# Sixteen-wide attention: the causal mask of the scores for the row minima, added by VectorE in the instruction that takes the minimum

## What is computed

```python
q = _rope(q, cos, sin); k = _rope(k, cos, sin)     # HEAD_DIM = 16, N_HEADS = 32, N_KV = 8
k = jnp.repeat(k, Q_PER_KV, axis=2)
v = jnp.repeat(v, Q_PER_KV, axis=2)
mask = _blocksparse_mask(S)                        # S = 1024: all causal pairs
scores = jnp.einsum('bqhd,bkhd->bhqk', q, k) * SM_SCALE
scores = jnp.where(mask[None, None], scores, jnp.finfo(scores.dtype).min)
probs = jax.nn.softmax(scores, axis=-1)
ctx = jnp.einsum('bhqk,bkhd->bqhd', probs, v).reshape(B, S, HIDDEN)
out = jnp.einsum('bsh,oh->bso', ctx, w_dense) + b_dense
```

## Time and profile before

| | |
|---|---|
| median of 3 runs | 2730.2 us (2727.94 to 2735.07) |
| span of the profiled execution | 2730.3 us |
| opening with fills, loop of `L0a` | 45 to 113 us, 113 to about 345 us |
| the same of `L1b` | from 2020 us, loop until about 2330 us |
| TensorE, VectorE, ScalarE, GpSimd busy | 93%, 70%, 55%, 32% |
| VectorE's reductions at L825, each attention | 304, 186.4 us |

### The profile page before, as it was taken

The page is one execution under the profiler, slowest core; times in us unless marked ns, Lnnn a source line. Parts: engine busy times, 40 slices in busy tenths (PEclk is TensorE's granted clock), DMA queues, the critical chain, the costliest instruction groups (busy, mean ns, idle before and its releaser), DMA issues. The chain is left out here.

```text
span 2730.3 us, 42122 instructions
## 1 busy us (share of the span) xinstructions
PE 2526.2 (93%) x14520; PEld 1768.8 (65%) x14582; DVE 1919.6 (70%) x3384; ACT 1497.2 (55%) x2530; POOL 879.1 (32%) x816
## 2 busy tenths in 40 slices
PE   7899989879999999999999988899778999898995
PEld 5444446757888888888888865566554444465663
DVE  6878734558777777777777677677578787376775
ACT  4677832335555555555555542566446778425663
POOL 2200014245444353434435320355312000014552
PEclk9799999989999999999999998999987999999998
DMA  4000000010000000000000003988820000149888
GB/s 177 1 1 1 1 21 1 1 51 17 24 20 20 24 24 20 24 16 24 17 24 24 13 21 140 345 198 198 197 74 1 1 1 2 66 177 301 199 197 210
DMA packets 68719, 196.24 MB, mean 72 GB/s; under 512 B 8960, under 2 KB 9728, under 8 KB 63392
## 3 DMA queue, kind: packets, MB, share of 16 engines
q1 hardware_dynamic: 47456, 144.25, 15.5%
q0 software_dynamic: 21056, 49.30, 9.7%
HBM read 153.14 MB, written 40.37 MB: 71 GB/s over the span
## 5 line engine op out<-in xcount | busy, mean ns | idle before, releaser
L1489 ACT ACTIVATE L1a_ph<-single 128x512 fp32r<-128x512 f32 (+3 forms) x384 | 174.3, 489 | 181.2 <-PE single L1574 180.5
L1480 ACT ACTIVATE L1a_probs<-pair,L1a_least 128x128 f32<-128x128 f32 (+7 forms) x256 | 189.9, 744 | 73.3 <-DVE L1a_least L1623 72.2
L1629 DVE TENSOR_TENSOR L1a_pl<-single,L1a_ph 128x512 fp32r<-128x512 f32 (+3 forms) x384 | 199.5, 549 | 42.7 <-ACT L1a_ph L1489 42.1
L1645 DVE SCALAR_TENSOR_TENSOR x<-single,L1a_rinv,x 128x512 f32<-128x512 f32 x256 | 189.4, 745 | 56.9 <-PE single L1230 56.6
L1457 POOL TENSOR_TENSOR L1a_swapped<-L1a_swapped,L1a_sin 128x512 f32<-128x512 f32 x80 | 129.2, 1616 | 301.0 <-ACT L1a_swapped L1521 301.0
L1623 DVE TENSOR_REDUCE L1a_least<-pair 128x1 f32<-128x128 f32 (+7 forms) x256 | 190.7, 750 | 42.9 <-PE pair L1563 42.3
L825 DVE TENSOR_REDUCE L1b_least<-single 128x1 f32<-128x512 f32 (+3 forms) x304 | 186.4, 657 | 37.8 <-PE single L647 20.3
L825 DVE TENSOR_REDUCE L0a_least<-single 128x1 f32<-128x512 f32 (+3 forms) x304 | 186.4, 657 | 37.6 <-PE single L647 19.2
L528 ACT ACTIVATE L1b_probsT<-pair 128x896 f32<-128x896 f32 (+2 forms) x192 | 149.0, 811 | 59.5 <-PE pair L667 47.2
L528 ACT ACTIVATE L0a_probsT<-pair 128x896 f32<-128x896 f32 (+2 forms) x192 | 148.9, 811 | 59.6 <-PE pair L667 47.3
L1574 PE MATMUL single<-ident,L1a_probs 128*128 128x128 f32 x1152 | 169.0, 274 | 0.4 <-ACT L1a_probs L1480 0.4
(11 more groups left out here) (537 smaller groups left out, 7023.9 us busy)
## 6 DMA issues: line engine op xcount, KB each, us to landing
L1f_wd<-in_L1f_w SPq DMA_DIRECT2D x48, 512.0 KB
L1g_wd<-in_L1f_w SPq DMA_DIRECT2D x48, 512.0 KB
L1a_raw<-in_L1a_w SPq DMA_DIRECT2D x80, 256.0 KB, 2.6
L1f_store<-in_L1f_w SPq DMA_DIRECT2D x16, 1024.0 KB, 10.2
L1g_store<-in_L1f_w SPq DMA_DIRECT2D x16, 1024.0 KB, 10.3
sum<-L0a_pad_row SPq DMA_DIRECT2D x2, 2304.0 KB, 17.1
sum<-x SPq DMA_DIRECT2D x16, 256.0 KB
x<-sum SPq DMA_DIRECT2D x16, 256.0 KB, 6.7
```

Of the source, the lines that this page charges most:

```text
L1480: act.activation(probs[:, u % 2, 0:n], g.pair[u % 2][:, 0:n], ACT.Exp, bias=least[:, u % 4:u % 4 + 1], scale=-1.0, accum_out=rsum[:, h % 2 ...
L1489: act.activation(p_tile(ph, u, i), turned_bank(u, i), ACT.Copy).then_inc(p_high, 1)
L1629: dve.tensor_tensor(p_tile(pl, u, i), turned_bank(u, i), p_tile(ph, u, i).bitcast(F32), ALU.subtract)\
L1645: dve.scalar_tensor_tensor(out=g.x[:, t, :], in0=aux_bank(("O", h, t)), scalar=rinv[:, h % 2, t:t + 1], in1=g.x[:, t, :], op0=ALU.mult, op ...
```

## The change

A new constant `later`, 128 x 512 in bf16, is zero but for its last 128 columns, which hold the mask. GpSimd builds it beside the other constants. TensorE's `fill` no longer issues the mask matmul. In `lowest`, an unmasked fill is read as before. For a masked one VectorE issues, per head, `tensor_tensor_reduce`: it adds the last w columns of `later` to the head's w columns in PSUM, writes the sum back in place, and puts the minimum into `least`.

```diff
@@ constants
+                pool.memset(g.later[:, :], 0.0).then_inc(done, 1)
...
+                pool.affine_select(out=g.later[:, HALF - P:HALF], in_=g.later[:, HALF - P:HALF], compare_op=ALU.is_ge,
+                                   fill=BIG, base=0, pattern=[[-1, P]], channel_multiplier=1).then_inc(done, 1)
@@ fill
-                        masked = part == banks_of(qt) - 1
                         mm = pe.matmul(to[:, o:o + w], a.qkT[0:KS, kv * GH + first + i, qt * P:(qt + 1) * P],
-                                       a.qkT[0:KS, kv + NH, k:k + w], start=True, stop=not masked)
-                        if masked:
-                            mm = pe.matmul(to[:, o + w - P:o + w], g.ident_b[:, :], g.mask_b[:, :],
-                                           start=False, stop=True)
+                                       a.qkT[0:KS, kv + NH, k:k + w], start=True, stop=True)
@@ lowest
-                    dve.tensor_reduce(a.least[:, part, qt, first:first + heads],
-                                      g.bank(BANK16["F", kv, f])[:, 0:heads * w].rearrange("p (j k) -> p j k", j=heads),
-                                      AX_X, ALU.min).then_inc(a.fill_read, 1)
+                    held = g.bank(BANK16["F", kv, f])
+                    if part == banks_of(qt) - 1:
+                        for i in range(heads):
+                            j = first + i
+                            mm = dve.tensor_tensor_reduce(out=held[:, i * w:(i + 1) * w], in0=held[:, i * w:(i + 1) * w],
+                                                          in1=g.later[:, HALF - w:HALF], scale=1.0, scalar=BIG,
+                                                          op0=ALU.add, op1=ALU.min, accum_out=a.least[:, part, qt, j:j + 1])
+                    else:
+                        mm = dve.tensor_reduce(a.least[:, part, qt, first:first + heads],
+                                               held[:, 0:heads * w].rearrange("p (j k) -> p j k", j=heads), AX_X, ALU.min)
+                    mm.then_inc(a.fill_read, 1)
```

More of the change, by code:

```diff
@@ L86, in __init__ @@
         self.mask_b = sb("mask_b", [P, P], BF16)
+        self.later = sb("later", [P, HALF], BF16)
         self.stats = sb("stats", [P, NT, 6])
@@ L209, in _ @@
                 pool.memset(g.ones[:, :], 1.0).then_inc(done, 1)
-                pool.wait_ge(done, 3)
+                pool.memset(g.later[:, :], 0.0).then_inc(done, 1)
+                pool.wait_ge(done, 4)
                 pool.affine_select(out=g.ident[:, :], in_=g.ident[:, :], compare_op=ALU.not_equal, fill=1.0,
@@ L215, in _ @@
                                    base=0, pattern=[[-1, P]], channel_multiplier=1).then_inc(done, 1)
-                pool.wait_ge(done, 5)
+                pool.affine_select(out=g.later[:, HALF - P:HALF], in_=g.later[:, HALF - P:HALF], compare_op=ALU.is_ge,
+                                   fill=BIG, base=0, pattern=[[-1, P]], channel_multiplier=1).then_inc(done, 1)
+                pool.wait_ge(done, 7)
                 pool.tensor_copy(g.ident_b[:, :], g.ident[:, :]).then_inc(done, 1)
-                pool.wait_ge(done, 6)
+                pool.wait_ge(done, 8)
 def fills():
```

## The result

| | before | after |
|---|---|---|
| median of 6 runs each, same chip | 2731.8 us (2726.0 to 2735.8) | 2720.6 us (2714.0 to 2725.6) |
| ratio | | 0.9962, 95% interval 0.9944 to 0.9979 |
| span of the profiled execution | 2730.3 us | 2718.3 us |

The changed kernel is faster by 0.4%, some 11 us, where the forecast was no change. The page of the changed kernel, part 1, answers to the earlier trace rows: TensorE has 18 us less work and VectorE 31 us more. 512 mask matmuls are gone, as the rows of weight loads (PEld, 14582 to 14070) count them; the matmul rows show 450, because before some were missing from the records.

The account below looks back on a forecast made before the run. TensorE was taken to bound the loop by its own work, VectorE to end last in the opening. Loop, opening and constant summed to 2 x (-1.4 + 1.65) + 0.2 = +0.7 us on 2730.3: forecast 2731 us, range 2713 to 2760.

Parts of the forecast that it names:

- VectorE's rate: Masked fills: the combined instruction runs at full rate, 0.07 us + 1.04 ns a column.
- the half-rate rival: Masked fills: the combined instruction costs 1.04 ns a column more, about 2845 us; chance 0.07, shared with a falling clock.
- The accumulator read, r = 0.08: VectorE, per head of a masked fill: the second instruction, reading the accumulator, adds r = 0.08 us, range 0.05 to 0.20.
- The dear-read rival: Fill 6 and opening: accumulator read costs over 0.12 us; 2749 us at 0.15, 2768 at 0.20; chance 0.28.
- The crowded run: Loop, fills 0 to 6: TensorE waits for VectorE at fills 3 to 6, +0.45 us a period.
- The rest of a period: Loop, after the crowded fills to fill 35: TensorE sheds 1.04 us, of which 0.65 is gained.
- The loop as a whole: Each attention's loop: seven periods at -0.2 us, -1.4 us in all (-4.2 to +3.2).
- The opening: First group of each attention: VectorE ends last, so its dearer fills add +1.65 us (0 to +3.2).
- The join: Between group 0's last minimum and the first copy of values: the forecast sum has no term for it.
- a falling clock: TensorE's clock falls because TensorE pauses: a slower outcome, chance 0.07 together with half rate.
- The total: Whole kernel: +0.7 us on 2730.3, forecast 2731 us; chance of the forecast case 0.50.
- Faster: TensorE's bound rules everywhere: Loop: what TensorE sheds arrives, 13 us per attention; all gives 2704 us, two thirds 2713; chance 0.15.

Follow-up runs that it names:

- both_masks: The changed kernel with TensorE's mask matmul put back into the fills, so the mask is added twice: 2738.5 us, ratio 1.0018.
- wide_fills_only: The combined instruction only in fills holding one head (384 and 512 columns), the others keeping TensorE's mask matmul as before: 2720.1 us, ratio 0.996.
- narrow_fills_only: The combined instruction only in fills holding two or four heads, the others keeping TensorE's mask matmul as before: 2733.2 us, one run.
- no_mask_in_first_pass: The kernel before without the first pass's mask matmuls, softmax shift being half the minimum over unmasked scores: 2709.5 us, ratio 0.9919.
- experiment 6: The kernel before with the combined instruction in group 0 alone, or in fills 0 to 10 of group 1 alone: 2733.1 and 2725.4 us, one run each.
- combined_but_in_the_crowd: The changed kernel with TensorE's mask put back at fills 0 to 2 of groups 2 to 7 alone: 2709.4 us, ratio 0.9928.
- opening_only: The kernel before with the combined instruction in the fills of group 0 alone: 2733.1 us, one run.
- constant_only: The kernel before with the new constant `later` built by GpSimd and not used: 2731.2 us, ratio 1.0001.

## Why the prediction was right about the loop and wrong about the sign

**VectorE's rate: right.** Rows of about 282, 415, 550 and 685 ns were forecast; they are 322, 458, 591 and 707. The rows are longer where an accumulator read lies beneath the start of the next. The distances of starts are those of the full rate, and the half-rate rival is out. The groups of VectorE by shape (busy us, mean ns, idle before), in both parts of the attention `L0a`:

```profile
L829 DVE CUSTOM_DVE_ANT_0 single<-single,later 128x512 f32<-128x512 f32 x64 | 43.9, 707 | 6.7 <-PE single L647 6.5
L829 DVE DVE_READ_ACCUMULATOR2_ANT L0a_least<- 128x1 f32 x256 | 36.3, 142 | 0.0
...
L829 DVE CUSTOM_DVE_ANT_0 single<-single,later 128x128 f32<-128x128 f32 x64 | 16.6, 322 | 0.7 <-PE single L647 0.7
```

The Trainium skill (Vector Engine (DVE) Microarchitecture Reference, Measured stream behaviour on trn2) would give the accumulator read the same 75 ns as any instruction in a row; the trace has 0.05 us.

**The accumulator read, r = 0.08: mis-sized, too dear.** It is 0.05, the low end of the range. A fill of 4 x 128 went from 0.60 to 1.00 us (four steps of 0.25; forecast 1.12), 2 x 256 to 0.76 (forecast 0.83), a wide one by 0.05 (forecast 0.08). Per period that is 2 x 0.40 + 4 x 0.16 + 16 x 0.05 = +2.2 us, not +3.2; over the first loop VectorE's work rose by 14.7 us (176.79 to 191.47) where 22 was forecast. The dear-read rival, priced from r = 0.12 up, falls.

**The crowded run: right in kind, and in size partly by luck.** TensorE waits for VectorE there, though at fills 3 and 6 alone, where the forecast had it wait at each of 3 to 6; the run costs +0.37 us a period, forecast +0.45. Two errors offset each other in that. By the prediction's own rule (0.10 us a period for each 0.01 on r) a read of 0.05 would have given +0.15. But the prediction let TensorE start the moment VectorE's next step could begin, and it starts later: the read of fill 3, whose bank fill 6 takes, begins at 210.47 and ends at 210.61, and fill 6 starts at 210.67. In all twelve waits it starts 0.20 us after the read's start and 0.06 after its end. So the read costs VectorE 0.05 us, but a bank comes free only after its whole row of 0.14.

**The rest of a period: right.** Forecast -0.65 of 1.04, measured -0.59 in the distance that has no crowded run. The share was a choice, and what keeps the remainder is not shown. The loop as a whole: -1.8 us per attention, forecast -1.4. The forecast counted seven crowded runs; there are six, and with six its own terms give 6 x 0.45 - 7 x 0.65 = -1.9.

**The opening: the step that failed.** It was put at +1.65 us per attention, on the ground that "there VectorE is what ends last". It came out at -0.8 and -1.0, and -2.0 and -2.5 with the join. This term alone turned a gain in both parts into a forecast of no change. Two things were wrong.

First, only the end of the opening was weighed, and TensorE's 32 matmuls were said to lie beside that. But up to 70 us TensorE's rows leave no gap (25.00 of 25.00 us from 25 to 50, 10.00 of 10.00 from 60 to 70). The window 50 to 60 us, before and, then, after (columns as in the earlier trace rows):

```profile
50.00:60.00 10.00, 10.00 (x85) 7.34 (x84) 7.96 (x20) 7.81 (x9) 1.40 (x1) 1.00 0.01 2
```
```profile
50.00:60.00 10.00, 10.00 (x81) 7.18 (x80) 8.34 (x22) 8.15 (x10) 1.41 (x2) 1.00 0.01 2
```

What it sheds there arrives whole, as the times show. Counted from the first bias add, the splits of VectorE (L815) begin at these times in `L0a`:

| mask matmuls ahead of the projection that feeds it | before | after | `both_masks` | shed x 0.058 |
|---|---|---|---|---|
| 4 | 34.30 | 34.06 | 34.30 | 0.23 |
| 8 | 42.54 | 42.06 | 42.54 | 0.46 |
| 11 | 50.33 | 49.68 | 50.33 | 0.64 |
| 13 (a bias add, L771) | 52.52 | 51.76 | 52.52 | 0.75 |
| end of the opening | 88.94 | 88.17 | 89.46 | |

0.24, 0.48, 0.65 and 0.76 us: one matmul at a time, and the lead is kept to the end. Two more kernels bear it out: `wide_fills_only` has shed none, none, 3 and 5 matmuls at these four places and leads by 0, 0, 0.16 and 0.29 us, `narrow_fills_only` has shed 4, then 8, and leads by 0.24, then 0.48. `both_masks`, with all of VectorE's extra work and TensorE's as before, keeps before's times there to 0.01 us: VectorE's extra costs nothing in this part. That fill 0's extra would be hidden ahead of the wait for GpSimd was right.

Second, the run at the end was misread. The opening was said to be "nearly without a pause" on VectorE from about 70 us, but two fills of this stretch had VectorE wait 0.80 us each for TensorE, before:

```profile
100.61 0.69 DVE L825 TENSOR_REDUCE L0a_least<-single 128x2 f32<-128x512 f32 x1 [0.80 <-PE single L647]
102.10 0.69 DVE L825 TENSOR_REDUCE L0a_least<-single 128x2 f32<-128x512 f32 x1 [0.80 <-PE single L647]
```

The row says x11 in 7.32 us; with the reduction after them, twelve took 8.12 us (105.77 to 113.89). The window over them, before:

```profile
105.77:113.89 8.12, 5.58 (x18) 1.26 (x18) 7.44 (x12) 2.17 (x2) 0.00 (x0) 0.71 0.00 0
```

Eight of 512 columns at 0.60 and four of 384 at 0.47 make 6.7. So 1.4 us beyond VectorE's own steps stood inside that row, in slivers too short to be printed. TensorE is busy 5.58 of the 8.12 us: the two engines hand two banks to and fro, and neither is full. From the last splits (70.35 after the first bias add) to the end before took 18.6 us, after 18.6 and 18.4, `no_mask_in_first_pass` 18.4, `both_masks` 19.1 and 19.0. VectorE's dearer instruction alone costs this hand-over some 0.4 to 0.5 us; taking the mask matmuls away gives 0.2 without it and 0.5 to 0.6 with it. The two together come out at nothing to 0.2 less.

**The join** was priced at nothing. It gave 1.2 and 1.5 us in the profiled execution, more by TensorE's clock than by its work (by the estimate of experiment 6, 1.0 and 1.3 of it). The prediction had a falling clock only as a mishap, and no rising one. That the short form came in both attentions of this execution is partly luck: six of the ten kernels with lighter openings had it in one alone.

**The total.** Forecast: 2 x (-1.4 + 1.65) + 0.2 = +0.7. By the same terms as measured: 2 x -1.8 for the loops, -1.8 for the openings, -2.8 for the joins, 0 for the constant, or -8.2 us; the medians differ by 11.2, with an interval of 6 to 15. With -0.8 for the opening and nothing for the join the forecast would have been 2726: the right sign, but a gain of 4 us, half of the 8.2 that the prediction took for what can be told from none.

**The rivals.** "Faster: TensorE's bound rules everywhere" gave 2704 to 2713. It did not hold in the crowded run. It is the right account of the opening's first half. `no_mask_in_first_pass` and `combined_but_in_the_crowd`, at 2709.5 and 2709.4, come near it, with part of what TensorE sheds still not arriving.

## What to carry to other kernels

Moving work from a full engine to one with room is worth what the full engine sheds only where the other has cover; where the two share a short ring of buffers, the same move can cost more than it brings, so decide it place by place (here three fills of 22 of a group, kept where they were, turned -8 us by stages into -17). When the bound of a stage is read from its last stretch, read the busy time of every engine in the earlier ones too, since what is shed there arrives as well. A merged row "x11 in 7.32 us" is not an engine without a pause until the count times the step of its shape says so.

## What the runs showed of the hardware that I had not expected

- The accumulator read behind a combined instruction has a row of 142 ns and costs 0.05 us of VectorE's time, because it starts with the next instruction. TensorE, waiting for the bank, starts 0.06 us after the end of that row, 0.20 after its start. A memset of one column (row 0.06) behind it cost nothing that the period shows beyond 0.06 us for 32 of them. A reduction of 16 columns cost 0.04.
- The combined add and minimum, f32 in PSUM written back in place and bf16 from SBUF, runs at 1.04 ns a column, as the plain reduction does.
- After a stretch at the lower clock, the same instructions took 7.3 or 8.6 us in one execution of one program (`opening_only`), by when the upper level was granted, 3.6 or 6.3 us into them.
- The opening repeats to 0.01 us between kernels (27.99, 34.30, 42.54, 50.33 us after the first bias add in before, `constant_only` and `both_masks`), and the loops of the four kernels with the same loop lie within 0.1 us (212.2 to 212.3). Two other kernels have loops that differ by 0.25 and 0.46 us between their two attentions. So in the openings and in most loops a difference of 0.05 us in one profiled execution can be read, while 29 runs of the kernel before on one chip lie between 2725.2 and 2741.3 us.
